# Two buffers for the first turns of x, and the second half of w3's gathers one turn later

## The chip, the cores and the metric

The kernel runs on one core of a Trainium2 chip. The metric is the device time of one execution in microseconds; the number to forecast is the median over runs of the changed kernel. One further execution was taken by the hardware profiler, and every row below comes from it.

## What is computed

The input x has 64 batches of 64 tokens with 512 features, float32. Four steps follow one another, each chosen per batch by an index: two low-rank adapters (4 and 8 experts, rank 16) around two dense 512x512 weights, and two mixes over the tokens, by one of 8 and one of 200 matrices of 64x64.

```python
x = x + _L0_cond_ref(x, W_base, Wt, A, B_w, Wp, scaling, itok_B_0_3)   # x W_base' + ((x Wt') A' B') Wp' * scaling
x = x + _L1_cond_ref(x, W, A, Bm, scalings, itok_B_0_6)                # x W' + (x A' B') * scaling
x = x + _L2_cond_ref(x, itok_B_0_7, weights2)     # einsum('bct,bcd->bdt', x, weights2[idx])
x = x + _L3_cond_ref(x, itok_B_1_198, weights3)   # the same with 200 matrices
```

Each is linear in x, and the token mixes commute with the feature steps. So the kernel forms one dense matrix g01 = (1 + W_base')(1 + W'), for each batch one 64x64 token matrix p = (1 + w2)(1 + w3), and for each batch a low-rank pair u (512x32) and v (32x512). Then y = p' x, z = u' y', and out = y g01 + z' v.

## The kernel before

A set-up of some 35 us builds g01 (as high and low float32r halves), the table u_tab in SBUF and the table v_table in DRAM. The 64 batches are then worked off in 8 turns of 4 pairs (`QUADS` = 8, `QUAD` = 4; a pair is two batches on 128 partitions). In TensorE's order turn i has these pieces:

- `token_mix(i)`: p of each batch, into y_ps; ScalarE copies it to `p_now` and adds one to `p_set`.
- `mix`: y of a half of the turn (h = 0 or 1, two pairs each) from `x_raw` and `p_now`, into y_ps; each pair adds one to `y_done`.
- `reduce`: z, from `u_sel` and `y_all`; `z_done`.
- `add_v(i)`: z times `v_sel` into o_ps; `v_done`. `v_ready` ahead of it waits for `z_set`, for both gathers of the turn (`v_in` at 32 (i + 1)) and for the banks to be read out.
- `apply(i, u)`: o of pair u, 12 matmuls of 512 columns over g01 (called "o of turn i" in the change); `o_done`.

`burst(i)` is token_mix(i+1), reduce of turn i, mix of turn i+1 and add_v(i). From turn 1 on the order is burst(i), then the four applies of turn i (`outputs`). Ahead of its reduce the burst waits for x of turn i+1 (`x_in`); before the last eighth of the reduce it waits for p (`p_set`).

VectorE copies y out of PSUM (`copy_y`), makes its low halves (`low_y`), places w2 (`place_w2`), adds the identity to w3 (`add_w3(i)`, which from turn 4 on waits for gathers 2 and 3 of w3), and reads out half of o (`copy_out`). ScalarE has the high halves, p, z and the other half of o. `copy_out` of turn i waits for the store of turn i-1 (`o_out`).

GpSimd (`@block.gpsimd`, L352) places u (`place_u`, 8 copies a half turn) and issues two kinds of indirect DMA. `fetch_v(i)` (L376) fetches v of turn i into `v_sel` with two gathers. v_sel has one buffer, so fetch_v(i) waits for `v_done` of turn i-1. `pick_w3(g)` (L369) gathers a quarter of the w3 matrices (16 batches) into `w3_pick[:, g]`, in rows of 2 KB.

SyncE (`@block.sync`, L242) issues all other loads and stores from one queue, and a wait in it holds all that stand behind. w3 goes by DRAM: `spill_w3(g)` (L292) stores w3_pick[:, g] to `w3_of`, and `load_w3(g)` (L298) loads it from there in another layout into `w3_all`. `load(i, h)` (L269) loads half a turn of x, 512 KB, into `x_raw`, which has one buffer; so it waits until the mix of the same half of turn i-1 is done. `store(i, h)` (L285) stores half of o. In a turn SyncE has store(i-1, 1), load(i+2, 1), load(i+2, 0), store(i, 0). `v_tab` (L134) is the SBUF staging of four parts of v_table: VectorE writes it once (L810) and SyncE stores it once (L317).

In the profile's names digits are left out: w3_pick reads as w_pick, w3_of as w_of, w3_all as w_all, and w3_now as w_now. x_raw, v_sel, o_ps and y_ps are as in the code. L853 is the line of `mm`, TensorE's helper, so its rows are told apart by tiles.

Of the kernel before, what the change touches and what calls it, by code (L numbers as in the profile page):

```python
# [11 lines left out]
PART = 128  # L12
BATCH = 64
SEQ = 64
D = 512
# [8 lines left out]
QUAD = 4  # L24
QUADS = PAIRS // QUAD
# [17 lines left out]
def build(nc, x, e0_ids, e1_ids, e2_ids, e3_ids, w_base, w_t, a0, b0, w_p, s0, w1, a1, b1, s1, w2, w3, out):  # L43
# [9 lines left out]
    with ctx:  # L53
# [28 lines left out]
        lane = sb("lane", [PART, 1], I32)  # L82
        w3_pick = sb("w3_pick", [PART, PICKS, SEQ * SEQ // PIECE])
        is_e2 = sb("is_e2", [PART, 2])
# [48 lines left out]
        v0g1 = sb("v0g1", [PART, D])  # L133
        v_tab = sb("v_tab", [PART, E1 // 2, D])  # L134
        u_tab = sb("u_tab", [PART, KC, E0 + E1, RANK])
        w2T = sb("w2T", [PART, E2, SEQ])
# [8 lines left out]
        w3_next = sb("w3_next", [PART, QUAD, SEQ])  # L145
        x_raw = sb("x_raw", [PART, QUAD, D])
        z = sb("z", [PART, 2, SEQ])
# [31 lines left out]
        p_done, p_set = sem("p_done"), sem("p_set")  # L179
        x_in = [sem(f"x_in{h}") for h in range(2)]  # L180
        y_done, yh_set, yl_set = sem("y_done"), sem("yh_set"), sem("yl_set")
# [31 lines left out]
        def y_of(u):  # L213

            at = D // 2 * (u % 2)
            return y_ps[:, u // 2 * 2:u // 2 * 2 + 2, at:at + D // 2].rearrange("p b (k t) -> p b k t", k=KC)

        p_bank = y_ps[:, 1, 0:QUAD * SEQ]
# [24 lines left out]
        def _(sp):  # L243
# [25 lines left out]
            def load(i, h):  # L269

                if isinstance(i, int) and i < 2:
                    wait(sp, y_done, 2 * i * (h + 1))
                else:
                    wait(sp, y_done, QUAD * (i - 1) + QUAD - 2 * h)
                sp.dma_start(x_raw[:, 2 * h:2 * h + 2, :],
                             x_rows[:, bass.ds(QUAD * i + 2 * h, 2), :]).then_inc(x_in[h], 16)

# [32 lines left out]
            load_w3(1)  # L310

            sp.wait_ge(setup_act, ACT_DONE["v1"])
            sp.dma_start(v_table[EF * RANK:, :], v1[:, :]).then_inc(table_out, 16)
            load(1, 0)
            for g in (2, 1, 3, 0):
                sp.wait_ge(setup_dve, DVE_DONE[f"v_{g}"])
                sp.dma_start(v_table[PART * g:PART * g + PART, :], v_tab[:, g, :]).then_inc(table_out, 16)  # L317
            load(1, 1)
            for g in range(2, PICKS):
                spill_w3(g)  # L320
            sp.wait_ge(v_in, 32)
            for h in (1, 0):
                load(2, h)
            for g in range(2, PICKS):
                load_w3(g)
            store(0, 0)

            def turn(i, more=True):
                store(i - 1, 1)
# [5 lines left out]
            with sp.Fori(1, QUADS - 2) as i:  # L335
                turn(i)
            turn(QUADS - 2, more=False)
            store(QUADS - 2, 1)

# [13 lines left out]
        def _(pool):  # L353
# [209 lines left out]
        def _(dve):  # L563
# [276 lines left out]
        def _(pe):  # L840
# [172 lines left out]
            def mix_ready(i, h):  # L1013

                pe.wait_ge(x_in[h], 16 * (i + 1))
                pe.wait_ge(p_set, i + 1)

            def mix(h):

                for u in range(2 * h, 2 * h + 2):  # L1020
                    for k in range(KC):
                        for half in range(2):
# [3 lines left out]
                            for b in range(2):  # L1026
                                rows = slice(SEQ * b, SEQ * b + SEQ)
                                last = mm(y_ps[to, 2 * h + b, col:col + SEQ], x_raw[rows, u, d:d + SEQ], p_now[rows, u, :],
                                          True, True)
# [83 lines left out]
            mix_ready(0, 0)  # L1113
            mix(0)
            g01_step(3, range(0, 2))
# [16 lines left out]
            pe.wait_ge(setup_dve, DVE_DONE["v_3"])  # L1132
            mix(1)
            token_ready(1)
# [8 lines left out]
            mix_ready(1, 1)  # L1143
            mix(1)
            mix_ready(1, 0)
            pe.wait_ge(z_set, 2)
            mix(0)
            apply(0, 2, first=True)
# [49 lines left out]
```

## Time and profile before

| what | us |
|---|---|
| median of 3 runs | 170.71 |
| lowest and highest run | 169.84, 171.48 |
| the profiled execution: device time | 169.73 |
| the profiled execution: span, first to last instruction | 168.0 |

The profiled execution has 1.7 us outside its span. It is 1.0 us under the median of the runs shown, just under the fastest of them. Sums are made against 169.73, and what they change is then taken off the median.

In the rows, PE is TensorE's matmuls, PEld its weight loads, DVE VectorE, ACT ScalarE, POOL GpSimd and SPq SyncE's queue. "issue" as a releaser means that the engine waited for nothing that the profile shows, and a wait for a DMA's semaphore can be among these. Two matmul records stand for one float32 matmul.

### The profile page before, as it was taken

The numbers are of one execution on the slowest core, as the hardware profiler recorded it, in microseconds if no ns is written. First come the engines' busy times: TensorE is split into PE (matmuls) and PEld (weight loads), VectorE is DVE, ScalarE is ACT, GpSimd is POOL, SyncE is SP. The second block draws the span as 40 slices with busy tenths as digits, with TensorE's granted clock in tenths as the row PEclk, the third lists the DMA queues.
The fourth block names the chain that finished last, engine by engine and source line by source line (L and its number), as shares of the span: only waits on it lengthen the run. The fifth ranks groups of instructions, "written<-read, shape, count | busy, mean of one in ns | idle before, by whom it ended". The sixth has DMA issues, their size and how long they took to land.

```text
span 168.0 us, 6390 instructions
## 1 busy us (share of the span) xinstructions
PE 160.4 (95%) x2365; PEld 124.9 (74%) x2365; DVE 92.9 (55%) x220; ACT 47.0 (28%) x90; POOL 57.2 (34%) x167
## 2 busy tenths in 40 slices
PE   5899999999989979999999999999999999999992
PEld 5678748758776848887888687788778886877782
DVE  4967766889757382348534842693386355423010
ACT  3234225481206202330332032221402420422110
POOL 4341110446750358007701840481067007500000
PEclk9999999999999999999999999999999999999999
DMA  4999786449577997308633833492177321333123
GB/s 149 302 342 325 226 228 214 129 161 329 162 234 241 307 342 245 127 29 258 219 125 124 277 100 125 165 303 114 44 265 234 125 98 47 111 125 129 62 79 108
DMA packets 21947, 30.79 MB, mean 183 GB/s; under 512 B 7272, under 2 KB 9704, under 8 KB 21928
## 3 DMA queue, kind: packets, MB, share of 16 engines
q1 hardware_dynamic: 20320, 25.31, 44.8%
q0 software_dynamic: 1600, 5.24, 10.7%
q8 instruction: 10, 0.16, 0.4%
q14 instruction: 9, 0.07, 0.1%
q10 hardware_dynamic: 8, 0.00, 0.0%
HBM read 19.80 MB, written 10.75 MB: 182 GB/s over the span
## 4 chain that ended last, share of the span: by engine, by line
PE 93%; DMA 3%; issue 1%; SPq 1%; POOL 0%; ACT 0%
PE o_ps L853 68%; PE y_ps L853 21%; DMA w_sb<-in_L_cond_W_dram 3%; PE y_ps L937 1%; PE y_ps L866 1%; PE y_ps L906 1%; PE y_ps L950 0%; SPq L250 0%; POOL w_sb L406 0%; SPq L253 0%; PE y_ps L981 0%; ACT o_sb L560 0%
## 5 line engine op out<-in xcount | busy, mean ns | idle before, releaser
L853 PE MATMUL o_ps<-g,yy 128*128 128x512 f32 (+1 forms) x384 | 89.0, 389 | 0.0
L853 PEld LDWEIGHTS o_ps<-g,yy 128*128 128x128 f32 x384 | 70.5, 188 | 20.3 <-issue 5.3
L392 POOL COPY u_sel<-u_tab 128x64 f32 x128 | 32.2, 271 | 61.8 <-PE o_ps L853 42.6
L723 DVE TENSOR_TENSOR yy<-y_all,yy 128x512 fp32r<-128x512 f32 x32 | 22.1, 697 | 27.0 <-ACT yy L483 26.8
L483 ACT ACTIVATE yy<-y_all 128x512 fp32r<-128x512 f32 x32 | 20.1, 629 | 52.1 <-issue 23.8
L763 DVE COPY o_sb<-o_ps 128x512 f32<-128x512 f32 x15 | 10.4, 691 | 22.4 <-PE o_ps L853 22.4
L716 DVE COPY y_all<-y_ps 128x512 f32<-128x512 f32 x32 | 19.9, 682 | 4.3 <-PE y_ps L853 4.3
L380 POOL DMA_INDIRECT v_sel<-v_table,v_rows x16 | 15.3, 959 | 11.1 <-PE o_ps L853 8.4
L853 PE MATMUL y_ps<-p_now,x_raw 64*64 64x64 f32 x1024 | 17.6, 220 | 0.9 <-issue 0.9
L853 PEld LDWEIGHTS y_ps<-p_now,x_raw 64*64 64x64 f32 x1024 | 16.1, 135 | 2.3 <-issue 1.7
L515 ACT ACTIVATE o_sb<-o_ps 128x512 f32<-128x512 f32 x16 | 9.4, 591 | 21.5 <-PE o_ps L853 17.6
L752 DVE COPY w_sel<-w2T 64x64 f32 x56 | 11.6, 219 | 4.3 <-issue 1.6
L853 PE MATMUL o_ps<-g,wb 128*128 128x512 f32 x48 | 12.6, 404 | 0.0
L853 PEld LDWEIGHTS o_ps<-g,wb 128*128 128x128 f32 x48 | 8.6, 188 | 2.6 <-issue 0.8
L853 PE MATMUL o_ps<-v_sel,z 32*64 32x512 f32 (+1 forms) x128 | 8.9, 606 | 1.2 <-issue 1.2
L853 PE MATMUL o_ps<-y_all,u_sel 128*32 128x64 f32 x384 | 6.9, 221 | 0.0
L853 PEld LDWEIGHTS o_ps<-y_all,u_sel 128*32 128x32 f32 x384 | 5.9, 109 | 0.5
L490 ACT ACTIVATE p_now<-y_ps 128x256 f32<-128x256 f32 x6 | 2.3, 384 | 13.7 <-PE y_ps L853 13.7
L371 POOL DMA_INDIRECT w_pick<-in_L_cond_weights_dram,spread x4 | 4.4, 1091 | 2.1 <-DVE spread L671 1.5
L898 PE MATMUL o_ps<-ident 128*128 128x128 f32 x12 | 3.0, 417 | 2.1 <-POOL ident L360 2.1
L445 ACT ACTIVATE g<-y_ps 128x512 fp32r<-128x512 f32 (+2 forms) x5 | 2.5, 511 | 8.4 <-PE y_ps L906 7.0
L401 POOL TENSOR_TENSOR wb_sb<-wb_sb,ident 128x128 f32<-128x128 f32 x4 | 1.9, 478 | 8.1 <-DMA wb_sb<-in_L_cond_W_base_dram 8.1
(119 smaller groups left out, 110.2 us busy)
## 6 DMA issues: line engine op xcount, KB each, us to landing
x_raw<-in_x_dram SPq DMA_DIRECT2D x16, 512.0 KB
out_dram<-o_sb SPq DMA_DIRECT2D x14, 512.0 KB, 3.1
w_sb<-in_L_cond_W_dram SPq DMA_DIRECT2D x4, 256.0 KB, 5.0
wb_sb<-in_L_cond_W_base_dram SPq DMA_DIRECT2D x4, 256.0 KB, 5.1
wp_sb<-in_L_cond_Wp_dram SPq DMA_DIRECT2D x2, 512.0 KB, 6.8
wt_sb<-in_L_cond_Wt_dram SPq DMA_DIRECT2D x1, 1024.0 KB, 10.6
w_of<-w_pick SPq DMA_DIRECT2D x4, 256.0 KB, 3.5
w_all<-w_of SPq DMA_DIRECT2D x4, 256.0 KB, 5.9
```

The source lines that it names most:

```text
L371: pool.indirect_dma_start(out=w3_pick[:, g, :], out_offset=None, in_=w3_pieces, in_offset=bass.IndirectOffsetOnAxis(ap=w3_rows[:, g, 0:1], ...
L380: pool.indirect_dma_start(out=v_sel[:, h, :], out_offset=None, in_=v_table, in_offset=bass.IndirectOffsetOnAxis(ap=v_rows[:, h, i:i + 1], ...
L392: nc.gpsimd.tensor_copy(u_sel[2 * h + u][:, :, b, RANK * part:RANK * part + RANK], u_tab[:, :, bass.ds(e, 1), :].rearrange("p k a r -> p k ...
L445: nc.scalar.activation(dst, src, ACT.Copy).then_inc(setup_act, 1)
L483: nc.scalar.activation(yy[u][:, :, 0, :], y_all[u][:, :, :], ACT.Copy).then_inc(yh_set, 1)
L515: nc.scalar.activation(o_sb[:, u, :], o_ps[u][:, :], ACT.Copy).then_inc(o_set, 1)
L716: nc.vector.tensor_copy(y_all[u][:, :, :].rearrange("p k (b t) -> p b k t", b=2), y_of(u)).then_inc(yf_set, 1)
L723: nc.vector.tensor_tensor(yy[u][:, :, 1, :], y_all[u][:, :, :], yy[u][:, :, 0, :].bitcast(F32), ALU.subtract).then_inc(yl_set, 1)
L752: nc.vector.tensor_copy(to[rows, u, :], w2T[rows, bass.ds(g, 1), :].rearrange("p a c -> p (a c)")).then_inc(w2_placed, 1)
L763: nc.vector.tensor_copy(o_sb[:, u, :], o_ps[u][:, :]).then_inc(o_set_dve, 1)
L853: return nc.tensor.matmul(dst, lhsT, rhs, start=start, stop=stop)
L898: nc.tensor.transpose(o_ps[3][:, 0:PART], ident[:, :], ident[:, :])
```

## The change

- x has two buffers, `x_even` for turns 0 and 2, and `x_odd` for turn 1 and every turn from 3 on. So x of turns 1 and 2 needn't wait for a buffer that is just being read, and load(3) waits for the mix of turn 1.
- SyncE issues load(1, .) behind load_w3(1), load(2, .) behind the stores of v_tab, and load(3, .) behind these. The wait of load(2, 1) for `v_in` is gone.
- Gathers 2 and 3 of w3 are issued by GpSimd after place_u(2, 1), and not ahead of fetch_v(0). Their spills and loads stand on SyncE behind store(0, 1), ahead of store(1, 0).
- w3_pick is the same memory as v_tab. VectorE waits for spills 0 and 1 before it writes v_tab.
- In `burst` the waits for x go from before the reduce to its last eighth, beside that for p.
- Each turn on SyncE now has its two loads ahead of both stores of that turn: load(i+2, 1), load(i+2, 0), store(i, 0), store(i, 1). With store(1, 1) ahead of the loop this is the order of before, cut at another place.

```diff
-        w3_pick = sb("w3_pick", [PART, PICKS, SEQ * SEQ // PIECE])
+        w3_pick = v_tab
-        x_raw = sb("x_raw", [PART, QUAD, D])
+        x_even = sb("x_even", [PART, QUAD, D])
+        x_odd = sb("x_odd", [PART, QUAD, D])
...
+        def x_of(i):
+            return x_even if isinstance(i, int) and i in (0, 2) else x_odd
...
             def load(i, h):
-                if isinstance(i, int) and i < 2:
-                    wait(sp, y_done, 2 * i * (h + 1))
+                if isinstance(i, int) and i < 4:
+                    if i >= 2:
+                        sp.wait_ge(y_done, 2 * h + 2 if i == 2 else 2 * QUAD - 2 * h)
                 else:
-                    wait(sp, y_done, QUAD * (i - 1) + QUAD - 2 * h)
+                    sp.wait_ge(y_done, QUAD * (i - 1) + QUAD - 2 * h)
...
+            for h in range(2):
+                load(1, h)
             sp.wait_ge(setup_act, ACT_DONE["v1"])
             sp.dma_start(v_table[EF * RANK:, :], v1[:, :]).then_inc(table_out, 16)
-            load(1, 0)
             for g in (2, 1, 3, 0):
                 sp.wait_ge(setup_dve, DVE_DONE[f"v_{g}"])
                 sp.dma_start(v_table[PART * g:PART * g + PART, :], v_tab[:, g, :]).then_inc(table_out, 16)
-            load(1, 1)
+            for h in range(2):
+                load(2, h)
+            for h in (1, 0):
+                load(3, h)
+            store(0, 0)
+            store(0, 1)
             for g in range(2, PICKS):
                 spill_w3(g)
-            sp.wait_ge(v_in, 32)
-            for h in (1, 0):
-                load(2, h)
             for g in range(2, PICKS):
                 load_w3(g)
-            store(0, 0)
+            store(1, 0)
+            store(1, 1)
...
             place_u(1, 0)
-            for g in range(2, PICKS):
-                pick_w3(g)
...
                 place_u(i + 1, 1)
+                if i == 1:
+                    for g in range(2, PICKS):
+                        pick_w3(g)
...
             dve.wait_ge(setup_act, ACT_DONE["v0g1_both"])
+            for g in range(2):
+                dve.wait_ge(w3_spilt[g], 16)
...
                 place_ready(i)
-                for h in range(2):
-                    pe.wait_ge(x_in[h], 16 * (i + 2))
                 pe.wait_ge(o_set, 2 * i - 1)
+                def x_ready():
+                    pe.wait_ge(p_set, i + 2)
+                    for h in range(2):
+                        pe.wait_ge(*x_in(i + 1, h))
                 reduce(o_ps[0], 0)
-                reduce(o_ps[0], 1, lambda: pe.wait_ge(p_set, i + 2)).then_inc(z_done, 1)
-                mix(1)
-                mix(0)
+                reduce(o_ps[0], 1, x_ready).then_inc(z_done, 1)
+                mix(i + 1, 1)
+                mix(i + 1, 0)
```

SyncE's queue from the store of v1 (v_table<-v) to its loop, before; the first x_raw row is load(1, 0), the second load(1, 1), the next two load(2, .):

```order
L313 DMA v_table<-v 128x512 [waits setup_act]
L275 DMA x_raw<-in_x_dram 128x2x512 [waits y_done]
L317 DMA v_table<-v_tab 128x512 [waits setup_dve] x4
L275 DMA x_raw<-in_x_dram 128x2x512 [waits y_done]
L295 DMA w_of<-w_pick 128x512 [waits w3_picked2]
L295 DMA w_of<-w_pick 128x512 [waits w3_picked3]
L275 DMA x_raw<-in_x_dram 128x2x512 [waits y_done,v_in]
L275 DMA x_raw<-in_x_dram 128x2x512 [waits y_done]
L301 DMA w_all<-w_of 128x8x64 [waits w3_spilt2]
L301 DMA w_all<-w_of 128x8x64 [waits w3_spilt3]
L289 DMA out_dram<-o_sb 128x2x512 [waits o_set_dve,o_set]
```

The same stretch now, from load(1, .) on:

```order
L288 DMA x_odd<-in_x_dram 128x2x512 x2
L328 DMA v_table<-v 128x512 [waits setup_act]
L331 DMA v_table<-v_tab 128x512 [waits setup_dve] x4
L288 DMA x_even<-in_x_dram 128x2x512 [waits y_done] x2
L288 DMA x_odd<-in_x_dram 128x2x512 [waits y_done] x2
L302 DMA out_dram<-o_sb 128x2x512 [waits o_set_dve,o_set] x2
L308 DMA w_of<-v_tab 128x512 [waits w3_picked2]
L308 DMA w_of<-v_tab 128x512 [waits w3_picked3]
L314 DMA w_all<-w_of 128x8x64 [waits w3_spilt2]
L314 DMA w_all<-w_of 128x8x64 [waits w3_spilt3]
L302 DMA out_dram<-o_sb 128x2x512 [waits o_set_dve,o_set] x2
```

Both loads of turn 1 moved ahead of v1's store, and four loads moved ahead of the first store of o. The two w_of stores, which wait for gathers 2 and 3, moved from ahead of load(2, .) to behind both stores of turn 0, and the stores of turn 1 stand behind w_all's loads.

GpSimd around fetch_v(0), before; the first row is the last copy of place_u(1, 0):

```order
L392 COPY u_sel<-u_tab 128x4x16
L371 DMA w_pick<-in_L_cond_weights_dram,spread 128x512 x2
L380 DMA v_sel<-v_table,v_rows 128x512 [waits v_rows_set,table_out,y_done]
L380 DMA v_sel<-v_table,v_rows 128x512
L387 TENSOR_LOAD ef_code [waits z_done]
```

The same place now:

```order
L408 COPY u_sel<-u_tab 128x4x16
L396 DMA v_sel<-v_table,v_rows 128x512 [waits v_rows_set,table_out,y_done]
L396 DMA v_sel<-v_table,v_rows 128x512
L403 TENSOR_LOAD ef_code [waits z_done]
L403 ISA x2
```

And now behind the last copy of place_u(2, 1), before GpSimd waits for the reduce of turn 2:

```order
L408 COPY u_sel<-u_tab 128x4x16
L387 DMA v_tab<-in_L_cond_weights_dram,spread 128x512 x2
L403 TENSOR_LOAD ef_code [waits z_done]
L403 ISA x2
L408 REGISTER_ALU
```

The two gathers (w_pick before, v_tab now) moved past fetch_v(0), place_u(1, 1), fetch_v(1), place_u(2, 0), fetch_v(2) and place_u(2, 1).

TensorE in burst(1), before, from token_mix(2) to the first matmul of add_v(1):

```order
L853 MATMUL y_ps<-w_now,w_sel 64x64 x8
L853 MATMUL o_ps<-y_all,u_sel 32x64 [waits x_in1,o_set,x_in0,u_placed]
L853 MATMUL o_ps<-y_all,u_sel 32x64 x27
L853 MATMUL o_ps<-y_all,u_sel 32x64 [waits p_set]
L853 MATMUL o_ps<-y_all,u_sel 32x64 x3
L853 MATMUL y_ps<-p_now,x_raw 64x64 x64
L853 MATMUL o_ps<-v_sel,z 64x512 [waits o_set,o_set_dve,v_in,z_set]
```

And now:

```order
L872 MATMUL y_ps<-w_now,w_sel 64x64 x8
L872 MATMUL o_ps<-y_all,u_sel 32x64 [waits o_set,u_placed]
L872 MATMUL o_ps<-y_all,u_sel 32x64 x27
L872 MATMUL o_ps<-y_all,u_sel 32x64 [waits x_even_in1,x_even_in0,p_set]
L872 MATMUL o_ps<-y_all,u_sel 32x64 x3
L872 MATMUL y_ps<-p_now,x_even 64x64 x64
L872 MATMUL o_ps<-v_sel,z 64x512 [waits o_set,o_set_dve,v_in,z_set]
```

Only the waits for x moved, from the first matmul of the reduce to one in its last eighth. The wait for v_in at add_v(1) is where it was.

## Rows read from the trace of the kernel before

**Rows 1.** The page: busy time, TensorE's clock in 40 slices, the chain's shares.

```profile
span 168.0 us, 6390 instructions
...
PE 160.4 (95%) x2365; PEld 124.9 (74%) x2365; DVE 92.9 (55%) x220; ACT 47.0 (28%) x90; POOL 57.2 (34%) x167
...
PEclk9999999999999999999999999999999999999999
...
PE 93%; DMA 3%; issue 1%; SPq 1%; POOL 0%; ACT 0%
```

**Rows 2.** TensorE's waits over the span: waited-for, us in total, times, longest.

```profile
PE o_ps L853 <- issue: 1.2, 1, 1.2
PE y_ps L853 <- issue: 0.9, 2, 0.5
```

**Rows 3.** The chain of waits in order of time: start us, us, what.

```profile
46.06 0.46 issue
...
46.80 0.43 issue
...
56.59 1.30 PE o_ps L853 x63
57.89 2.02 PE y_ps L853 x128
59.92 1.15 issue
...
73.69 1.06 PE o_ps L853 x64
...
89.33 1.06 PE o_ps L853 x64
```

**Rows 4.** GpSimd's timeline: start us, us, instruction, idle before it.

```profile
41.58 0.98 POOL L371 DMA_INDIRECT w_pick<-in_L_cond_weights_dram,spread  x1 [0.15 <-issue]
42.86 1.28 POOL L371 DMA_INDIRECT w_pick<-in_L_cond_weights_dram,spread  x1 [0.31 <-issue]
...
54.27 0.97 POOL L380 DMA_INDIRECT v_sel<-v_table,v_rows  x1 [4.03 <-PE o_ps L853]
55.54 0.95 POOL L380 DMA_INDIRECT v_sel<-v_table,v_rows  x1 [0.30 <-issue]
...
64.90 1.95 POOL L392 COPY u_sel<-u_tab 128x64 f32 x8
```

**Rows 5.** DMA issues and packets, windows 55.5 to 55.9, 63.9 to 64.4, 79.6 to 80.

```profile
DMA packets 406, 0.12 MB, mean 291 GB/s; under 512 B 405, under 2 KB 405, under 8 KB 405
...
v_sel<-v_table,v_rows POOLq DMA_INDIRECT x1, 5.4
...
v_sel<-v_table,v_rows POOLq DMA_INDIRECT x1, 4.2
...
v_sel<-v_table,v_rows POOLq DMA_INDIRECT x1, 4.6
```

**Rows 6.** Stretches of 3 us: busy time by engine, clock, DMA share, GB/s.

```profile
62.00:65.00 3.00, 3.00 (x21) 2.38 (x14) 1.23 (x6) 0.00 (x0) 2.01 (x3) 1.00 0.91 292
65.00:68.00 3.00, 3.00 (x15) 2.49 (x14) 0.80 (x2) 1.16 (x3) 1.86 (x8) 1.00 0.48 162
```

**Rows 7.** SyncE's queue in order of time.

```profile
54.34 3.23 SPq L289 DMA_DIRECT2D out_dram<-o_sb  x2
59.22 1.29 SPq L275 DMA_DIRECT2D x_raw<-in_x_dram  x2
...
76.06 1.92 SPq L275 DMA_DIRECT2D x_raw<-in_x_dram  x2
```

**Rows 8.** DMA issues in 46.3 to 47: KB each, us to landing.

```profile
w_of<-w_pick SPq DMA_DIRECT2D x1, 256.0 KB, 4.3
```

**Rows 9.** VectorE's timeline, turn 2.

```profile
80.86 0.41 DVE L736 TENSOR_TENSOR w_now<-w_all,ident 128x256 f32<-128x256 f32 x1
```

**Rows 10.** The tile w3_pick: all its DMAs, landing.

```profile
DMA to landing us min/median/max: 3.0/4.3/7.7
```

More of the change, by code:

```diff
@@ L179, in build @@
         p_done, p_set = sem("p_done"), sem("p_set")
-        x_in = [sem(f"x_in{h}") for h in range(2)]
+        x_even_in = [sem(f"x_even_in{h}") for h in range(2)]
+        x_odd_in = [sem(f"x_odd_in{h}") for h in range(2)]
         y_done, yh_set, yl_set = sem("y_done"), sem("yh_set"), sem("yl_set")
@@ L216, in y_of, with x_in @@
             return y_ps[:, u // 2 * 2:u // 2 * 2 + 2, at:at + D // 2].rearrange("p b (k t) -> p b k t", k=KC)
+        def x_of(i):
+            return x_even if isinstance(i, int) and i in (0, 2) else x_odd
+        def x_in(i, h):
+            if isinstance(i, int) and i in (0, 2):
+                return x_even_in[h], 16 * (i // 2 + 1)
+            return x_odd_in[h], 16 if isinstance(i, int) and i == 1 else 16 * (i - 1)
         p_bank = y_ps[:, 1, 0:QUAD * SEQ]
@@ L269, in load @@
             def load(i, h):
-                if isinstance(i, int) and i < 2:
-                    wait(sp, y_done, 2 * i * (h + 1))
-                else:
-                    wait(sp, y_done, QUAD * (i - 1) + QUAD - 2 * h)
-                sp.dma_start(x_raw[:, 2 * h:2 * h + 2, :],
-                             x_rows[:, bass.ds(QUAD * i + 2 * h, 2), :]).then_inc(x_in[h], 16)
+                if isinstance(i, int) and i < 4:
+                    if i >= 2:
+                        sp.wait_ge(y_done, 2 * h + 2 if i == 2 else 2 * QUAD - 2 * h)
+                else:
+                    sp.wait_ge(y_done, QUAD * (i - 1) + QUAD - 2 * h)
+                sp.dma_start(x_of(i)[:, 2 * h:2 * h + 2, :],
+                             x_rows[:, bass.ds(QUAD * i + 2 * h, 2), :]).then_inc(x_in(i, h)[0], 16)
             def store_last(u):
@@ L317, in _ @@
                 sp.dma_start(v_table[PART * g:PART * g + PART, :], v_tab[:, g, :]).then_inc(table_out, 16)
-            load(1, 1)
+            for h in range(2):
[4 more added lines that the diff above has]
+            store(0, 1)
             for g in range(2, PICKS):
                 spill_w3(g)
-            sp.wait_ge(v_in, 32)
-            for h in (1, 0):
-                load(2, h)
             for g in range(2, PICKS):
                 load_w3(g)
-            store(0, 0)
+            store(1, 0)
+            store(1, 1)
             def turn(i, more=True):
-                store(i - 1, 1)
                 if more:
@@ L333, in turn @@
                 store(i, 0)
-            with sp.Fori(1, QUADS - 2) as i:
+                store(i, 1)
+            with sp.Fori(2, QUADS - 2) as i:
                 turn(i)
             turn(QUADS - 2, more=False)
-            store(QUADS - 2, 1)
             for u in range(QUAD - 1):
@@ L1013, in mix_ready, with mix @@
             def mix_ready(i, h):
-                pe.wait_ge(x_in[h], 16 * (i + 1))
+                pe.wait_ge(*x_in(i, h))
                 pe.wait_ge(p_set, i + 1)
-            def mix(h):
+            def mix(i, h):
                 for u in range(2 * h, 2 * h + 2):
@@ L1027, in mix @@
                                 rows = slice(SEQ * b, SEQ * b + SEQ)
-                                last = mm(y_ps[to, 2 * h + b, col:col + SEQ], x_raw[rows, u, d:d + SEQ], p_now[rows, u, :],
+                                last = mm(y_ps[to, 2 * h + b, col:col + SEQ], x_of(i)[rows, u, d:d + SEQ], p_now[rows, u, :],
                                           True, True)
@@ L1113, in _ @@
             mix_ready(0, 0)
-            mix(0)
+            mix(0, 0)
             g01_step(3, range(0, 2))
@@ L1132, in _ @@
             pe.wait_ge(setup_dve, DVE_DONE["v_3"])
-            mix(1)
+            mix(0, 1)
             token_ready(1)
@@ L1143, in _ @@
             mix_ready(1, 1)
-            mix(1)
+            mix(1, 1)
             mix_ready(1, 0)
             pe.wait_ge(z_set, 2)
-            mix(0)
+            mix(1, 0)
             apply(0, 2, first=True)
```

## The prediction

> **What bounds the kernel now.** I read the page first. TensorE's matmuls are busy for 160.4 of 168.0 us, at full clock in each of the 40 slices, and the chain that ended last is 93% TensorE [rows 1]. So an edit to loads can give only what TensorE spends waiting. Next I read TensorE's waits. In the turns there are two places: 1.2 us ahead of a matmul into o_ps, and 0.9 us in two pieces ahead of matmuls into y_ps [rows 2]. The chain in order of time says where. The 1.15 us begin at 59.92, right behind the mix of burst(1) (57.89 + 2.02), which is add_v(1). The two small ones, 0.46 and 0.43, lie at 46.06 and 46.80, inside mix(1, 1) [rows 3]. A third loss is hidden in a busy piece: the reduce of burst(1) takes 1.30 us, that of burst(2) and of burst(3) 1.06 each [rows 3]. From 61.07 on TensorE's chain shows no wait up to the last matmuls. In all the early turns hold 1.15 + 0.89 + 0.24 = 2.28 us that a change of DMA traffic could give back, 1.3% of the time. That is the ceiling of the gain.
>
> The releaser of the 1.15 us reads "issue", so the cause has to be found elsewhere. add_v(1) waits for both gathers of fetch_v(1). GpSimd can issue them only when add_v(0) has let go of v_sel: at 54.27 and 55.54 [rows 4]. The second took 5.4 us to land [rows 5], so it was there at 60.9, and TensorE went on at 61.07. Gathers of other turns took 4.2 and 4.6 us [rows 5]. In turn 1 they meet w3's last loads: in 55.5 to 55.9, 405 of 406 packets are under 512 B, at 291 GB/s [rows 5]. In later turns the fetch is issued some ten us ahead of its use, so only turn 1 is tight.
>
> **The change part by part.**
>
> 1. *x of turns 1 and 2 loaded sooner.* In before no x load is the last thing that TensorE waits for, so this gives nothing by itself. The new buffer doesn't help add_v(1) either. Its use is that the 1 MB of load(3), issued from 59.22 on in before [rows 7], goes out when mix(1) is done, from about 48.5 to 49.5, and has landed before fetch_v(1) is issued. Cost of the early load(1): v1's store waits behind two issues, about 1 us. Its cover is the stores of v_tab, which come later and which fetch_v(0) waits for in any case. Value 0. From below, if the table is late by 1 us, fetch_v(0) has 2.8 us in hand from part 2, so 0 there too. x can't be late for turn 1: it is asked for some 15 us before mix(1, 1).
>
> 2. *Gathers 2 and 3 taken from 41.58 to 44.14 on GpSimd* [rows 4]. fetch_v(0) goes out up to 2.8 us sooner. Its result is used at about 52, and TensorE doesn't wait there in before; value 0. fetch_v(1) is bound by add_v(0) and is issued at 54.27 as before.
>
> 3. *w3's spills and loads 2 and 3 leave 44 to 58.* This is the part that pays. From 54.3 to 60 only the two stores of o, 1 MB, are left beside fetch_v(1). The second gather then lands like one of the other turns: 55.54 + 4.2 = 59.7, or + 4.6 = 60.1, against 59.92 for the end of the mix. The wait is 0 to 0.25 us, less the shift of next part. I take 0.1 left of 1.15: gain 1.05. The bounds are 1.15 (all of it), and 0 if gathers take 5.4 us whatever runs beside them.
>
> 4. *The reduce of burst(1).* If its slow 0.24 us come from the same traffic, they go: 1.30 becomes 1.06. The waits for x, put later inside it, cost nothing: they are passed already. I take the 0.24; bounds 0 and 0.24.
>
> 5. *The two gaps at 46 us.* There SyncE has the spills, and GpSimd has fetch_v(0). Both are gone or sooner now, but at 39 us 1 MB of load(2) is new in the queue, and load(3) is new at 49. The trace doesn't say what TensorE lacked. Value 0; bounds -0.89 (both gone) and +0.89 (as much again).
>
> 6. *The same work, put into turns 1 and 2.* VectorE's new wait for spills 0 and 1 is passed at once, since both are some 6 us old when it writes v_tab. For the rest I follow the queues. place_u(2, 1) ends at 64.90 + 1.95 = 66.85 in before [rows 4], and at 65.7 when add_v(1) is 1.15 us sooner. The picks are issued at 65.9 and 67.2 (1.28 apart at 41.58 [rows 4]). With the median landing of 4.3 [rows 10] the second is in at 71.5. SyncE has been waiting for it with store(1, 0), store(1, 1) and load(4, .) behind. The spill takes 4.3 [rows 8]: 75.8. Then w3's load, both stores and load(4, .) go out in about 2 us, up to 78, where before has load(4, .) from 76.06 on [rows 7]. How long do these 3 MB take, with fetch_v(3) among them? The same set (w3's load, two stores, a fetch, two x loads) ran in before from 54.34, its first store [rows 7]. After 65 the DMA engines are busy at 0.48 of 3 us [rows 6], so it was over by 65 + 1.4 = 66.4, after 12.1 us at most. That gives 87.9 here. Who waits? TensorE wants x of turn 4 in the last eighth of the reduce of burst(3): 89.33 + 7/8 of 1.06 = 90.3 in before [rows 3], 88.9 with 1.3 us gained. ScalarE's copy_out(2, 0) waits for store(1, 0), with high_y(3, 1) behind it, and the reduce of burst(3) wants it from 88.0. add_w3(4), at 80.86 in before [rows 9], would run at some 83, and its user token_mix(4) comes just ahead of that reduce, at 87.6. All of it fits, the tightest by 1 us, and 12.1 is a bound from above. Value 0; bounds 0 and +2.4 (below).
>
> Sum: -1.05 - 0.24 = -1.3 us. The profiled execution would come to 169.73 - 1.3 = 168.4. Off the median of the runs shown it is 170.71 - 1.3 = 169.4, 0.8% faster.
>
> **The rivals.**
>
> *The early gaps close as well.* The spills at 44 to 47 were part of the trouble, and with light traffic TensorE runs through. Against it: 1 MB of load(2) has taken their place nearby. -1.3 - 0.89 = -2.2: 168.5.
>
> *The gather isn't freed.* Its 5.4 us may be mostly its own: its two gathers follow one another, and the stores of o are still there. For it: the first fetches in rows 5 differ among themselves by 0.4 us with no small packets near, so contention isn't their only term. Against it: both are at least 0.8 us under 5.4 while x was being loaded beside them. The gain is the 0.24 us at most: 170.5. What a rule makes of this: by the Trainium skill, "DMA: Bandwidth & Descriptors", section "Queues, rings and completion order", each DMA engine goes round-robin between the queue rows that have work, a packet at a time. So a backlog on SyncE's row wouldn't hold the gather's row by its length, and taking w3's load out would leave the gather its turns between stores as before. By that rule the sum is this rival's. The rows bear it out only in part, since the gather's time did change with what lay beside it.
>
> *SyncE stands still too long* (the slower side). Place: the wait for gather 3 in turn 1, with load(4, .) behind it. A gather took up to 7.7 us to land [rows 10]. Then the spill goes at 67.2 + 7.7 = 74.9, w3's load at 79.2, and x of turn 4 is in at 91.3 instead of 88.9. TensorE waits 2.4 us in burst(3), where it has no slack: -1.3 + 2.4 = +1.1, 171.8. It decides from the point where w3's last load is issued later than 76.8. For it: the margin is 1 us by the bound. Against it: the 7.7 us was met at the start, when the weights filled the queue, and the bound of 12.1 is generous.
>
> *The change doesn't do what it says* would mean that x wasn't what anyone waited for. That is my own reading in part 1, and it costs the forecast nothing.
>
> **How the numbers follow.** The forecast (about -1.3, from -0.8 to -1.7) has 0.50, the closed gaps 0.24, the gather not freed 0.12, SyncE's standstill 0.14. A measurement of this kernel tells about 1% from no change, here 1.7 us: under 169.0 is faster, over 172.4 slower. Faster: 0.24 and 0.09 from the forecast's edge, 0.33. Slower: the worse half of the standstill, 0.08, for it can cost more than 2.4 where spill and stores are slow too. Within 1%: the rest, 0.59. The range goes from 168.0, just under the closed gaps, to 171.9, just over the priced standstill.
>
> **What would show it.** Right: no wait ahead of add_v(1), the second gather of fetch_v(1) landing in 4 to 4.6 us, the reduce of burst(1) at 1.06 us, and no packets under 512 B in 54 to 60 but many in 75 to 80. Wrong: a gather of over 4.6 us with only stores beside it; a wait in burst(3) ahead of the mix or in its reduce; add_w3(4) later than 87; or, for part 5, the gaps at 46 us gone or grown. If the median falls by more than 2.3 us, my ceiling is wrong, and time outside the waits of the profiled execution was at stake.

## The result and the profile after

| | before | changed |
|---|---|---|
| median | 170.28 (4 runs, 169.18 to 171.48) | 167.91 (4 runs, 167.62 to 168.48) |
| ratio, 95% interval | 1 | 0.985 [0.981, 0.989] |
| profiled execution's span | 168.0 | 166.3 |

The change makes the kernel 1.5% faster, 2.4 us by the medians and 1.7 us by the two profiled executions. The page of the changed kernel: span, busy time, clock, the chain's shares.

```profile
span 166.3 us, 6376 instructions
...
PE 161.5 (97%) x2365; PEld 125.6 (75%) x2365; DVE 92.2 (55%) x220; ACT 47.2 (28%) x90; POOL 57.5 (35%) x167
...
PEclk9999999999999999999999999999999999999999
...
PE 97%; POOL 1%; issue 0%; ACT 0%; POOLq 0%
```

TensorE's waits now, over the whole span:

```profile
PE o_ps L917 <- POOL ident L376: 2.1, 1, 2.1
```

Both early waits of [rows 2] are gone, the 1.2 us and the 0.9 us; one at the start is all that is left. The chain in order of time (start us, us, what):

```profile
45.77 2.61 PE y_ps L872 x160
48.38 6.93 PE o_ps L872 x40
...
55.71 1.29 PE o_ps L872 x62
56.99 2.02 PE y_ps L872 x128
59.02 12.15 PE o_ps L872 x64
...
71.57 1.23 PE o_ps L872 x64
...
87.36 1.23 PE o_ps L872 x64
...
150.14 1.03 PE y_ps L872 x64
```

The two sides of each stretch can be set off against one another. In before the mix of burst(1) ended at 59.92 and TensorE went on at 61.07 [rows 3]; here it ends at 59.01 and goes on at 59.02. The reduce of burst(1), at 55.71, took 1.29 us against 1.30: nothing was won there. But that of burst(2), at 71.57, and of burst(3), at 87.36, is now 1.23, where [rows 3] had 1.06. By stretches of TensorE's chain:

| stretch | before | changed | difference |
|---|---|---|---|
| start to the first applies | 39.51 | 40.11 | +0.60 |
| the first applies, to 45.17 and 45.77 | 5.66 | 5.66 | 0 |
| second reduce of turn 0 and mix(1), to 49.27 and 48.38 | 4.10 | 2.61 | -1.49 |
| applies and add_v(0), reduce and mix of burst(1) | 10.65 | 10.64 | -0.01 |
| wait at add_v(1) | 1.15 | 0 | -1.15 |
| from there to the reduce of turn 7 (five loop turns) | 90.35 | 91.12 | +0.77 |
| the rest, to the end of the span | 16.58 | 16.16 | -0.42 |
| sum | | | -1.70 |

The 1.15 came back at the place that the forecast named. fetch_v(1)'s two gathers landed in (us, min, median, max)

```profile
DMA to landing us min/median/max: 4.0/4.3/4.6
```

against 5.4 for the second in [rows 5], with few small packets beside them in 54 to 58:

```profile
DMA packets 444, 1.08 MB, mean 270 GB/s; under 512 B 40, under 2 KB 40, under 8 KB 444
```

(in the same window before had 2105 packets under 512 B). GpSimd's indirect DMAs:

```profile
42.58 0.97 POOL L396 DMA_INDIRECT v_sel<-v_table,v_rows  x1 [0.57 <-issue]
43.86 0.95 POOL L396 DMA_INDIRECT v_sel<-v_table,v_rows  x1 [0.31 <-issue]
...
53.38 0.97 POOL L396 DMA_INDIRECT v_sel<-v_table,v_rows  x1 [4.18 <-PE o_ps L872]
54.66 0.94 POOL L396 DMA_INDIRECT v_sel<-v_table,v_rows  x1 [0.30 <-issue]
...
65.52 0.98 POOL L387 DMA_INDIRECT v_tab<-in_L_cond_weights_dram,spread  x1 [0.16 <-issue]
66.80 1.21 POOL L387 DMA_INDIRECT v_tab<-in_L_cond_weights_dram,spread  x1 [0.30 <-issue]
```

fetch_v(0) is issued at 42.58 and 43.86, and so is done when mix(1) begins at 46.3. In before the four gathers ran one behind the other from 41.58, the last of them at about 45.7, beside mix(1). The two at 65.52 and 66.80 are w3's. SyncE's queue around their spills, and add_w3(4) on VectorE:

```profile
68.69 1.95 SPq L308 DMA_DIRECT2D w_of<-v_tab  x2
71.93 1.00 SPq L314 DMA_DIRECT2D w_all<-w_of  x2
73.02 1.14 SPq L302 DMA_DIRECT2D out_dram<-o_sb  x2
74.56 2.74 SPq L288 DMA_DIRECT2D x_odd<-in_x_dram  x2
```

```profile
79.55 0.54 DVE L753 TENSOR_TENSOR w_now<-w_all,ident 128x256 f32<-128x256 f32 x1
```

w3's last load is issued by 72.9 (71.93 + 1.00), where the forecast had 75.8, and load(4, .) from 74.56 on. TensorE waited for none of it. But the gathers of fetch_v(3), issued at 76.39 and 77.67 behind w3's loads and two stores, with load(4, .) around them, took 6.2 and 6.1 us to land, against 4.3 and 4.6 for the same fetch in before. Packets and landing in 76 to 80:

```profile
DMA packets 771, 1.40 MB, mean 349 GB/s; under 512 B 99, under 2 KB 99, under 8 KB 771
...
v_sel<-v_table,v_rows POOLq DMA_INDIRECT x2, 6.2
```

w3's own small packets lay ahead of that, in 72 to 76 (2029 of 2201 under 512 B). So a gather is slow here with few small packets beside it.

### The profile page after: what moved, and what is told of

It reads as the page before. It is cut to its first block, busy times and chain, and to the rows that moved or that the text cites. A ratio compares the mean times of both kernels' runs of the same rounds, so it can differ in the third digit from the quotient of the medians.

```text
span 166.3 us, 6376 instructions
## 1 busy us (share of the span) xinstructions
PE 161.5 (97%) x2365; PEld 125.6 (75%) x2365; DVE 92.2 (55%) x220; ACT 47.2 (28%) x90; POOL 57.5 (35%) x167
## 3 DMA queue, kind: packets, MB, share of 16 engines
q1 hardware_dynamic: 20320, 25.31, 45.7%
## 4 chain that ended last, share of the span: by engine, by line
PE 97%; POOL 1%; issue 0%; ACT 0%; POOLq 0%
PE o_ps L872 70%; PE y_ps L872 21%; PE o_ps L917 2%; PE y_ps L956 1%; PE y_ps L885 1%; PE y_ps L925 1%; PE y_ps L931 0%; PE y_ps L969 0%; PE y_ps L1000 0%; ACT o_sb L577 0%; POOL ident L376 0%; POOL piece L373 0%; PE y_ps L934 0%; POOL ident L371 0%; POOL owner L374 0%
## 5 line engine op out<-in xcount | busy, mean ns | idle before, releaser
L408 POOL COPY u_sel<-u_tab 128x64 f32 x128 | 32.4, 273 | 60.6 <-PE o_ps L872 40.1
L500 ACT ACTIVATE yy<-y_all 128x512 fp32r<-128x512 f32 x32 | 20.1, 629 | 51.1 <-PE o_ps L872 23.7
L872 PE MATMUL o_ps<-g,wb 128*128 128x512 f32 x48 | 13.4, 424 | 0.0
L872 PE MATMUL y_ps<-p_now,x_odd 64*64 64x64 f32 x768 | 12.6, 220 | 0.0
L872 PEld LDWEIGHTS y_ps<-p_now,x_odd 64*64 64x64 f32 x768 | 11.7, 135 | 0.5
L872 PE MATMUL o_ps<-y_all,u_sel 128*32 128x64 f32 x384 | 7.9, 222 | 0.0
L387 POOL DMA_INDIRECT v_tab<-in_L_cond_weights_dram,spread x4 | 4.3, 1076 | 1.4 <-DVE spread L688 0.8
```

The lines of the kernel that those rows point to most:

```text
L387: pool.indirect_dma_start(out=w3_pick[:, g, :], out_offset=None, in_=w3_pieces, in_offset=bass.IndirectOffsetOnAxis(ap=w3_rows[:, g, 0:1], ...
L408: nc.gpsimd.tensor_copy(u_sel[2 * h + u][:, :, b, RANK * part:RANK * part + RANK], u_tab[:, :, bass.ds(e, 1), :].rearrange("p k a r -> p k ...
L500: nc.scalar.activation(yy[u][:, :, 0, :], y_all[u][:, :, :], ACT.Copy).then_inc(yh_set, 1)
L872: return nc.tensor.matmul(dst, lhsT, rhs, start=start, stop=stop)
```

## The experiments

Kernels that were tried together ran on one chip and share its runs of before (e1 to e4, e5 to e8, e9); ratios are to these, whose medians are 171.58 us (e1 to e4), 171.01 (e5 to e8) and 170.34 (e9). In the table, "mix(1)" is the stretch from the second reduce of turn 0 to the end of mix(1); "loop" is from the start of turn 1's applies, or of the add_v ahead of them, to the reduce of turn 7.

| run | mix(1) | wait at add_v(1) | loop | median | ratio to before |
|---|---|---|---|---|---|
| before | 4.10 | 1.15 | 90.35 | 170.28 | 1 |
| changed | 2.61 | 0 | 91.12 | 167.91 | 0.985 [0.981, 0.989] |
| e1 before again | 4.06 | 2.32 | 90.36 | 170.93 | 0.996 [0.992, 1.000] |
| e2 changed, x waits ahead | 2.61 | 0 | 90.39 | 167.40 | 0.976 [0.971, 0.981] |
| e3 changed, w3 back | 5.73 | 0.65 | 91.20 | 171.38 | 0.995 [0.991, 1.000] |
| e4 before, w3 moved | 2.81 | 0 | 90.29 | 166.53 | 0.972 [0.967, 0.977] |
| e5 before, spills late | 4.19 | 0.07 | 90.35 | 167.85 | 0.981 [0.977, 0.986] |
| e6 e4, fetch_v(0) held back | 5.19 | 0 | 90.28 | 169.60 | 0.993 [0.990, 0.996] |
| e7 e2, w3_pick apart | 2.61 | 0 | 90.41 | 166.77 | 0.975 [0.971, 0.979] |
| e8 e4 again | 2.83 | 0 | 90.31 | 166.66 | 0.974 [0.971, 0.978] |
| e9 e4, x waits late | 2.61 | 0 | 91.15 | 167.71 | 0.985 [0.981, 0.989] |

The start, up to the first applies, lies between 39.0 and 40.1 us over these kernels, and differs by 1.0 us between e4 and e8, which are the same kernel. In e1, e2 and e4 nearly all of the difference lies between 5.7 and 8.4 us: four matmuls that read the first weights take 1.39, 1.97 and 1.17 us there. So the +0.60 of the result's table is no effect of the change that these runs show.

**e1: the kernel before once more.** No edit.

> The kernel before once more, to see which of its early waits recur. Theory (the changed kernel's gain is 1.15 us at add_v(1) and 1.5 us in mix(1), both caused by the placing of w3's gathers 2 and 3 and their spills and loads): both recur, the wait ahead of add_v(1) at 0.8 to 1.3 us, and mix(1) takes 4.1 us from the reduce of turn 0 to its end instead of 2.6. Rival (the gap in mix(1) is chance, as of an instruction fetch): it is gone or at another place. Time 1.00 times before for both.

The chain at the two places:

```profile
46.58 0.46 issue
...
59.70 2.32 issue
```

Both waits recur at their places, the second gap of mix(1) at 46.58, so neither is chance. But the wait at add_v(1) is 2.32 us here, twice that of the first profile. fetch_v(1)'s gathers landed in

```profile
DMA to landing us min/median/max: 5.5/6.1/6.6
```

So the size of this wait varies from one execution to another; what it varies with isn't shown. 1.15 was one sample of it.

**e2: the changed kernel, the waits for x ahead of the reduce.**

```diff
-                def x_ready():
-                    pe.wait_ge(p_set, i + 2)
-                    for h in range(2):
-                        pe.wait_ge(*x_in(i + 1, h))
+                for h in range(2):
+                    pe.wait_ge(*x_in(i + 1, h))
...
-                reduce(o_ps[0], 1, x_ready).then_inc(z_done, 1)
+                reduce(o_ps[0], 1, lambda: pe.wait_ge(p_set, i + 2)).then_inc(z_done, 1)
```

> The changed kernel with the waits for x ahead of the reduce again, as before, and only that for p in its last eighth. Theory (the reduce in the loop went from 1.06 to 1.23 us by the register instruction and waits put inside it): 1.06 again in each of 5 loop turns, 0.85 us under the changed kernel, so 0.98 times before. Rival (the reduce is slower for another reason, as the new tiles of x or the code's place): 1.23 stays, 0.985 times before. x itself isn't late in either, so no wait appears ahead of the reduce.

```profile
45.76 2.61 PE y_ps L872 x160
...
71.54 1.06 PE o_ps L872 x64
```

The reduce at 71.54 takes 1.06 us again, the loop 90.39 us instead of 91.12, and no wait for x has come in. In the order of the loop's instructions the changed kernel has a register instruction between the reduce's 28th and 29th matmul; here it stands ahead of the first:

```
changed:
REGISTER_ALU [waits p_set]
MATMUL o_ps<-y_all,u_sel 32x64 [waits x_odd_in1,x_odd_in0]
e2:
REGISTER_ALU [waits o_set]
MATMUL o_ps<-y_all,u_sel 32x64 [waits x_odd_in1,x_odd_in0]
```

The register instruction and two more waits inside a run of small matmuls cost 0.17 us a turn, though TensorE waits for no semaphore there. In burst(1), which stands ahead of the loop, the order of instructions has the two waits at this place and no register instruction, and its reduce takes 1.18, 1.20 and 1.29 us with them (e3, e9, changed) and 1.24 to 1.31 without. That points at the register instruction, but no run has it alone.

**e3: the changed kernel, w3's part undone.**

```diff
             pool.wait_ge(table_out, 16 * (1 + E1 // 2))
+            for g in range(2, PICKS):
+                pick_w3(g)
...
-                if i == 1:
-                    for g in range(2, PICKS):
-                        pick_w3(g)
...
             for h in range(2):
                 load(2, h)
+            for g in range(2, PICKS):
+                spill_w3(g)
             for h in (1, 0):
                 load(3, h)
+            for g in range(2, PICKS):
+                load_w3(g)
             store(0, 0)
             store(0, 1)
-            for g in range(2, PICKS):
-                spill_w3(g)
-            for g in range(2, PICKS):
-                load_w3(g)
```

> The changed kernel with the w3 part undone: gathers 2 and 3 ahead of fetch_v(0), their spills and loads ahead of the stores of o. x keeps its two buffers and early loads. Theory (w3's place is what pays, x's early loads alone give nothing): the wait of about 1.1 us at add_v(1) and the 1.5 us in mix(1) are back, some 2.4 us over the changed kernel, 1.00 times before. Rival A (x's early loads pay, for load(3) is out of the way of fetch_v(1)): the wait at add_v(1) stays away, 1.5 us over the changed kernel or less. Rival B (fetch_v(0) and the gap at 46 us hang on load(1) or load(2), not on w3): the gap in mix(1) stays away.

TensorE's waits in the turns:

```profile
PE y_ps L871 <- issue: 1.6, 4, 0.4
PE o_ps L871 <- DMA v_sel<-v_table,v_rows: 0.9, 1, 0.9
PE o_ps L871 <- issue: 0.7, 1, 0.7
```

and GpSimd's indirect DMAs, the first two w3's, the others fetch_v(0):

```profile
43.38 1.36 POOL L387 DMA_INDIRECT v_tab<-in_L_cond_weights_dram,spread  x1 [1.99 <-DMA v_table<-v_tab]
45.04 0.95 POOL L387 DMA_INDIRECT v_tab<-in_L_cond_weights_dram,spread  x1 [0.30 <-issue]
46.29 0.95 POOL L396 DMA_INDIRECT v_sel<-v_table,v_rows  x1 [0.30 <-issue]
47.54 0.95 POOL L396 DMA_INDIRECT v_sel<-v_table,v_rows  x1 [0.30 <-issue]
```

With w3's part undone next to nothing of the gain is left (0.995 times before), though x has its two buffers and early loads. The gap in mix(1) is larger than before's, 5.73 us for the stretch. One difference to before is my own: the gathers have to wait for v_tab here, since they share its memory, and so all four go out 1.8 us later. fetch_v(0) then lands late and add_v(0) waits for it (the 0.9 and 0.7 us hold that wait and the one at add_v(1), 0.65). The wait at add_v(1) is 0.65 us, smaller than in before, and the gathers of fetch_v(1), issued later, land in at most 5.0 us. So this run alone doesn't shut out that x's early loads pay for a part (rival A). e4, which has no wait without them, shows that they aren't needed.

**e4: the kernel before with w3's part alone.** x_raw has one buffer and w3_pick memory of its own.

```diff
             load(1, 1)
-            for g in range(2, PICKS):
-                spill_w3(g)
             sp.wait_ge(v_in, 32)
             for h in (1, 0):
                 load(2, h)
-            for g in range(2, PICKS):
-                load_w3(g)
             store(0, 0)
+            store(0, 1)
+            for h in (1, 0):
+                load(3, h)
+            for g in range(2, PICKS):
+                spill_w3(g)
+            for g in range(2, PICKS):
+                load_w3(g)
+            store(1, 0)
...
-            with sp.Fori(1, QUADS - 2) as i:
+            with sp.Fori(2, QUADS - 2) as i:
...
             place_u(1, 0)
-            for g in range(2, PICKS):
-                pick_w3(g)
...
                 place_u(i + 1, 1)
+                if i == 1:
+                    for g in range(2, PICKS):
+                        pick_w3(g)
```

> The kernel before with the w3 part alone: gathers 2 and 3 after place_u(2, 1), their spills and loads on SyncE behind load(3, .) and ahead of store(1, 0), w3_pick with memory of its own. x has one buffer and its old loads. Theory (w3's place is what pays): no wait at add_v(1), or under 0.3 us, and no gap in mix(1); the reduce in the loop stays at 1.06, so 2.4 us or so under before, 0.985, and 0.8 us better than the changed kernel if x isn't late. Rival A (x's part is needed too): at least one of the two waits stays, 0.99 to 1.00 times before.

```profile
44.68 2.81 PE y_ps L858 x158
...
58.10 12.15 PE o_ps L858 x64
...
70.64 1.06 PE o_ps L858 x64
```

From 44.68 on mix(1) runs through, add_v(1) follows at once (54.84 + 1.24 + 2.02 = 58.10), and the reduce is 1.06. It is the fastest kernel of the study, 0.972 times before and, on another chip as e8, 0.974. That is more than the 0.985 expected: before is slower on these two chips than beside the changed kernel, while e4 and e8 stay within 0.13 us of one another. Of the change only w3's move pays. x's second buffer and its early loads aren't needed for either wait.

**e5: only the spills and loads of w3 late, its gathers where they were.** e4's edit on SyncE, and none on GpSimd.

```diff
-            for g in range(2, PICKS):
-                spill_w3(g)
             sp.wait_ge(v_in, 32)
...
+            store(0, 1)
+            for h in (1, 0):
+                load(3, h)
+            for g in range(2, PICKS):
+                spill_w3(g)
+            for g in range(2, PICKS):
+                load_w3(g)
+            store(1, 0)
```

> The kernel before with gathers 2 and 3 of w3 where they were on GpSimd, and only their spills and loads on SyncE behind load(3, .), ahead of store(1, 0). Theory (the wait at add_v(1) comes from w3's loads in packets of 256 B beside fetch_v(1); the gap in mix(1) comes from GpSimd issuing indirect DMAs beside the 64x64 matmuls): no wait at add_v(1) or under 0.3 us, the gap of 0.9 us in mix(1) stays, 0.982 times before. Rival for the gap (the spills' traffic at 45 to 50 us): the gap goes too, 0.972 times before. Rival for the wait (the w3 gathers delay the chain of fetches): the wait stays, 0.99 or more.

TensorE's wait in the turns, GpSimd's issue of fetch_v(0), and fetch_v(1)'s landing:

```profile
PE y_ps L857 <- issue: 0.9, 2, 0.5
```

```profile
44.21 0.95 POOL L384 DMA_INDIRECT v_sel<-v_table,v_rows  x1 [0.30 <-issue]
45.46 0.95 POOL L384 DMA_INDIRECT v_sel<-v_table,v_rows  x1 [0.30 <-issue]
```

```profile
DMA to landing us min/median/max: 4.3/4.5/4.7
```

This separates the two waits. The one at add_v(1) is 0.07 us and its gathers land in at most 4.7 us, so w3's spills and loads made it. Whether by their small packets or by their mere bytes in SyncE's queue, this run doesn't tell, and fetch_v(3) of the changed kernel (6.2 and 6.1 us, 99 of 771 packets small) speaks for the second at least in part. The 0.9 us in mix(1) stay, with no spill near, so the spills' traffic didn't make that gap. The gathers on GpSimd did, or the fetch_v(0) that they push beside mix(1).

This run also tells more of the size. Its median is 3.2 us under before's on the same chip, with mix(1) and the loop as in before. Less the 0.4 us at the end that every edit shows (below), the wait at add_v(1) was some 2.8 us in a typical execution on that chip, an estimate that leaves out the start.

**e6: e4, with fetch_v(0) held back until the reduce of turn 0 is done.** No gather of w3 is near.

```diff
             pool.wait_ge(v_rows_set, 4)
+            pool.wait_ge(z_done, 2)
             fetch_v(0)
-            pool.wait_ge(z_done, 2)
             place_u(1, 1)
```

> The kernel before with the w3 part (as in e4), and fetch_v(0) held back on GpSimd until the reduce of turn 0 is done, so that its two gathers are issued beside mix(1). Nothing of w3 is near. Theory (indirect DMAs being issued starve TensorE's 64x64 matmuls): mix(1) takes 1 us or more longer than e4's 2.8, in small gaps whose releaser is issue, until some 0.6 us after GpSimd has issued the second gather. Rival (w3's own gathers or spills made the gap): mix(1) as in e4. In both add_v(0) waits 1 to 2 us, since v of turn 0 lands later, and fetch_v(1) moves with it; so the time is 0.98 to 0.99 times before, and the trace decides.

The chain in mix(1), and GpSimd's two gathers of fetch_v(0):

```profile
46.91 0.12 issue
47.03 0.35 PE y_ps L858 x5
47.38 0.40 issue
47.78 0.31 PE y_ps L858 x3
48.09 0.44 issue
48.53 0.33 PE y_ps L858 x3
48.87 0.43 issue
49.29 0.92 PE y_ps L858 x39
```

```profile
46.43 0.98 POOL L384 DMA_INDIRECT v_sel<-v_table,v_rows  x1 [5.16 <-PE y_ps L858]
47.71 0.95 POOL L384 DMA_INDIRECT v_sel<-v_table,v_rows  x1 [0.30 <-issue]
```

The gap is back, and larger. Between 46.91 and 49.29 TensorE gets through 11 matmul records in three bursts with some 0.4 us between them, and the stretch takes 5.19 us instead of e4's 2.81. w3 has no part in it, and neither has data in flight. The DMA engines' packets in 46.9 to 48.0, with two of the gaps in it, are

```profile
DMA packets 0, 0.00 MB, mean 0 GB/s; under 512 B 0, under 2 KB 0, under 8 KB 0
```

GpSimd has issued its second gather at 48.66, and TensorE runs on freely from 49.29, 0.6 us later. In all, 0.6 to 0.7 us lie between the end of GpSimd's last issue and TensorE's last gap in before, e1, e3 and e5. Where the issues end before mix(1) starts (changed, e2, e4, e7, e8, e9), there is no gap; in e4 and e8 the stretch is still 0.2 us longer than the 2.61 of the others, for no reason that is shown. The expected wait at add_v(0) didn't come: its gathers landed in 3.2 and 3.4 us, by 51.1, before TensorE, late by mix(1), was there. The median was 0.993 times before, above the 0.98 to 0.99 expected; of the 2.9 us over e8 on the same chip, mix(1) explains 2.4.

A rival isn't settled by this. The DMA view lists two queues of the kind "instruction", q8 and q14, and each has a packet near this stretch, at 47.6 and 49.4 in before, 46.4 and 46.8 in e6, 47.0 and 47.4 in changed. So the issues of GpSimd may hold TensorE up by way of a fetch of instructions, or at another place. No run tells these apart.

**e7 and e8: does x's part cost?** e7 is e2 with w3_pick in memory of its own and without VectorE's wait for the spills; e8 is e4's kernel.

```diff
-        w3_pick = v_tab
+        w3_pick = sb("w3_pick", [PART, PICKS, SEQ * SEQ // PIECE])
...
-            for g in range(2):
-                dve.wait_ge(w3_spilt[g], 16)
```

> The kernel of e2 (the changed kernel with the waits for x ahead of the reduce) with w3_pick in memory of its own, so without VectorE's wait for spills 0 and 1. Theory (x's two buffers and early loads and the shared memory are all neutral): the same as e4 within 0.3%, both 0.972 to 0.976 times before. Rival A (x's early loads cost 0.9 us, as the medians of e2 and e4 would have it): this as e2, 0.5% over e4. Rival B (the shared memory costs it): this as e4, and e2 was slower by the sharing.

> The kernel of e4 once more, beside e7 on one chip. Both theories: 0.972 times before again, no wait of over 0.3 us in TensorE's turns, reduce in the loop 1.06 us. Compared with e7: equal within 0.3% if x's part is neutral, 0.5% faster if the early loads cost.

166.77 and 166.66 us, 0.1% apart, on one chip. x's two buffers and early loads are neutral. The shared memory seems to be so: e2 and e7, which differ in it alone, have 0.976 and 0.975, but on two chips. In the profiled executions of e2 and e4 the start differs by 1.07 us, which is all of their difference in span (1.0 us); of the 0.9 us between their medians that is the likely reason, not a shown one.

**e9: e4 with the waits for x late, as the changed kernel has them.** The reverse of e2's edit, on e4.

```diff
-                for h in range(2):
-                    pe.wait_ge(x_in[h], 16 * (i + 2))
                 pe.wait_ge(o_set, 2 * i - 1)
+                def x_ready():
+                    pe.wait_ge(p_set, i + 2)
+                    for h in range(2):
+                        pe.wait_ge(x_in[h], 16 * (i + 2))
...
-                reduce(o_ps[0], 1, lambda: pe.wait_ge(p_set, i + 2)).then_inc(z_done, 1)
+                reduce(o_ps[0], 1, x_ready).then_inc(z_done, 1)
```

> The kernel of e4 (before with the w3 part alone) with the waits for x moved into the last eighth of the reduce, as the changed kernel has them. Theory (that place costs by the register instruction that comes to stand inside the reduce): the reduce in the loop takes 1.23 us instead of 1.06 in each of 5 turns, 0.8 us over e4 and e8 in the stretch of the loop, 0.977 to 0.98 times before. Rival (the 1.23 of the changed kernel came from its other edits, and the late wait is free): 1.06 and 0.973 as e4 and e8.

```profile
71.39 1.23 PE o_ps L858 x64
```

The reduce takes 1.23 us, the loop 91.15 instead of e4's 90.29 and e8's 90.31, so this edit costs 0.85 us in the loop, 0.5% of the time. The ratio is 0.985 against 0.972 and 0.974, which looks like more than 1%, but each of these stands on the before of another chip (170.34, 171.58 and 171.01). The medians themselves are 167.71 against 166.53 and 166.66, 1.1 to 1.2 us apart.

## Why the prediction was wrong, and where it was right

I forecast 169.4, 0.8% faster, and gave 168.0 to 171.9; it came to 167.91, just below, and 1.4% faster than 170.28 by the medians, 1.5% by the ratio. The sign and the part on the wait at add_v(1) were right. The step that failed is the value 0 for moving GpSimd's gathers and for the gaps at 46 us (2 and 5 below), which measured 1.49 us together. By the prediction's steps:

1. *x loaded sooner is worth nothing by itself*: right, shown by e7 beside e8. But I went on to say that its use is to have load(3) out of fetch_v(1)'s way. That was wrong. e4 has load(3) where it was, and no wait.
2. *Gathers taken from GpSimd: value 0*: wrong, and this is the main step that failed. I looked at who waits for fetch_v(0)'s data, and nobody does. What it costs is where it is issued. The picks pushed it beside mix(1), and there the issuing held TensorE: the stretch took 4.10 us and now takes 2.61. e5 shows that the gap comes with the gathers, e6 that fetch_v(0) beside mix(1) makes it without w3.
3. *w3's spills and loads leave: -1.05*: that they make the wait was right (e5: wait 0.07 us, landings of 4.3 to 4.7). That it is their small packets was my reading, and isn't shown. The term was mis-sized, for I took the 1.15 of one execution as the wait. e1 has 2.32, and the medians of e5 say some 2.8. The change took off all of it.
4. *The reduce of burst(1): -0.24*: wrong. It stayed at 1.29, and was 1.18 to 1.31 in all runs, w3 near or not. w3's spills and loads aren't what slows it. GpSimd ends issuing fetch_v(1) just ahead of it in all of them, and in e6 issues beside mix(1) did hold TensorE up, but no run moved these, so it is a guess.
4b. *The waits for x, put later, cost nothing*: wrong. They cost 0.17 us in each of five turns, 0.73 to 0.86 in the loop (e2, e9). I asked only whether the semaphore would be set. In the loop the order of instructions has a register instruction in the middle of the reduce, and I gave it no price.
5. *The gaps at 46 us: value 0, down to -0.89*: the value was wrong, and the bound too. The stretch lost 1.49 us. The profile's idle time of 0.89 leaves out that the few matmuls between the gaps were slow as well (2 records in 0.29 us, where 128 take 2.02). So my ceiling of 2.28 us was wrong too, as the sign that I gave for it (a fall of over 2.3 us) says: the median fell by 2.4.
6. *The same work in turns 1 and 2: value 0*: right. The picks landed in 3.2 and 3.5 us, not 4.3, and w3's small packets ran in 72 to 76, not 75 to 80. So the margin was larger than the 1 us of the bound. fetch_v(3) took 6.2 and 6.1 us by it, but it has some ten us in hand.

In the profiled executions the errors of 4b and 5 stood against one another: -1.49 and +0.77 where I had nothing. With step 3 at its measured 1.15 and step 4 at 0 that makes -1.88, and with +0.60 at the start and -0.42 at the end the measured -1.70. The -0.42 at the end is not explained: from TensorE's last matmul to the end of the span before and e1 have 3.0 us, and all kernels with an edit 2.6. The medians moved by 2.4 us rather than 1.7. The wait of step 3, which varies and is only in before, is the likely reason: e1's 2.32 and the estimate from e5 fit it. The clock is another: beside e1 to e4, six of 17 executions of before show a granted clock of 0.987 to 0.99 and spans of 170.1 to 171.2 us, the other eleven 1.0 and 168.6 to 170.7. For the unprofiled runs of before in the result neither is shown.

Of the rivals, the one that came true is the closing of the early gaps, at 168.5. Its mechanism as I put it (the spills' traffic) is refuted by e5, and that its number came near is partly luck: the gaps gave 0.6 us more than it had, the late waits took back 0.77. SyncE's standstill and the gather that isn't freed didn't come, the latter by landings of 4.0 to 4.6 us. The round-robin rule of the Trainium skill ("DMA: Bandwidth & Descriptors", "Queues, rings and completion order") had spoken for it. What I drew from the rule, that a backlog on SyncE's queue doesn't hold the gather by its length, isn't what the runs show. The slower gather of fetch_v(1) landed in 5.4 and 6.6 us with w3's loads queued beside it (before, e1), in 4.6 and 4.7 without (changed, e5), and fetch_v(3) went from at most 4.6 to 6.2 when w3's loads moved beside it.

## What to carry to other kernels

Ask of a DMA that GpSimd issues not only who waits for its data, but also what TensorE does while it is being issued: beside 128x512 matmuls it was free here (5.66 us for 24 of them in before, with three issues beside them, and in e6, with none), beside 64x64 ones the stretch took 4.1 to 5.7 us instead of e4's 2.8. A wait whose semaphore is always set still has a price where it splits a run of small matmuls inside a loop; put it ahead of the run if nothing is lost by it. And where a change has several parts, run each alone: one of three made the gain here (2.64 us of the chain in the profiled executions), one took 0.77 of it back, and e4, with the gain alone, has medians 1.3 to 1.4 us under the changed kernel's (e8 and e4, each on another chip).

## What the runs showed of the hardware

- Indirect DMAs being issued by GpSimd and 64x64 float32 matmuls don't go well together: gaps of 0.4 us, up to 4 of them, ending 0.6 to 0.7 us after the last issue (before, e1, e3, e5, e6). It is not data in flight: in e6 no packet moved in 46.9 to 48.0 while TensorE stood still, and in the changed kernel the second gather landed at 47.2 with mix(1) running from 46.3 without a gap. What TensorE lacks in the gaps (its releaser reads "issue") isn't shown.
- A 256 KB gather of GpSimd landed in 3.1 to 4.8 us in most turns, and in 5.0 to 7.2 us in some, most of them with w3's spills or loads, stores and loads of x issued shortly before (6.6 in e1, 7.1 in e3, 7.2 in e2). The size of the packets doesn't explain it alone: 6.2 us in changed with 99 of 771 under 512 B. The wait for it varied between two executions of the same kernel, 1.15 and 2.32 us; the other stretches of the chain repeat within 0.05 us, but for the start.
- One register instruction and two passed waits in the middle of a run of matmuls of 64 columns over 128x32 weights cost TensorE 0.17 us, the same in 15 turns of three kernels (changed, e3, e9).
- A granted clock of 0.977 to 0.99 shows in 15 of the 73 executions of before, e1, e3 and e6 on three chips, and in none of the 34 of the other kernels, all at 0.998 or more. What lowers it isn't shown; e5, which keeps the gap in mix(1), is among the 34 with four executions.
